# Layer 0's experts with down products five steps behind the up products

## The reference

```python
router_probs = softmax(flat @ router_w + router_b)          # 8 experts
topk_probs, topk_idx = top_k(router_probs, 2)
weights = zeros_like(router_probs).at[rows, topk_idx].add(topk_probs)
shared_out = gelu(flat @ sw1 + sb1) @ sw2 + sb2              # hidden width 256
h1 = gelu(einsum('td,edh->teh', flat, rw1) + rb1)            # all 8 experts
expert_out = einsum('teh,ehd->ted', h1, rw2) + rb2
return shared_out + einsum('ted,te->td', expert_out, weights)
```

## Time and profile before

| | |
|---|---|
| median of 3 runs | 460.7 us |
| profiled execution | 462.43 us, span 460.6 us |
| busy in the span | PE 411.1 (89%), DVE 359.3 (78%), ACT 334.5 (73%), POOL 253.1 (55%) |
| layer 0's experts | 65.8 to about 201 us: tiles of 31.0, 35.4, 35.9 and 32.9 us |
| PE idle in that stage, by its waits | 12 waits for hidl or hidh, 9.8 us together |
| granted TensorE clock over the span | 0.974 |

### The profile page before, as it was taken

The page is one execution under the profiler, slowest core; times in us unless marked ns, Lnnn a source line. Parts: engine busy times, 40 slices in busy tenths (PEclk is TensorE's granted clock), DMA queues, the critical chain, the costliest instruction groups (busy, mean ns, idle before and its releaser), DMA issues.

```text
span 460.6 us, 7995 instructions
## 1 busy us (share of the span) xinstructions
PE 411.1 (89%) x2340; PEld 276.2 (60%) x2340; DVE 359.3 (78%) x891; ACT 334.5 (73%) x898; POOL 253.1 (55%) x276
## 2 busy tenths in 40 slices
PE   8989778899799899889788888979999999999995
PEld 6667566586577667554333333434467787887883
DVE  4768795767898969867988898889966798778763
ACT  4276558798687686677999989999974575675552
POOL 3302238696876677750253446354538875666663
PEclk9899999899999999995999899989999999999999
DMA  6721021131133545561325545421316343432640
GB/s 183 220 74 43 0 76 64 46 95 46 48 113 93 128 122 164 114 109 46 103 47 87 123 116 85 98 74 23 104 27 170 118 138 101 130 114 99 194 123 23
DMA packets 45675, 44.70 MB, mean 97 GB/s; under 512 B 5556, under 2 KB 33788, under 8 KB 45632
## 3 DMA queue, kind: packets, MB, share of 16 engines
q1 hardware_dynamic: 45632, 44.19, 36.1%
HBM read 37.73 MB, written 6.44 MB: 96 GB/s over the span
## 4 chain that ended last, share of the span: by engine, by line
PE 30%; DVE 14%; ACT 7%; DMA 7%; SPq 3%; issue 3%; POOL 1%; POOLq 0%; DVEq 0%; ACTq 0%
PE P L1255 7%; PE P L1257 7%; PE P L1256 7%; DVE nm L911 6%; ACT EX L1192 5%; SPq L342 3%; DMA G<-gate_rows 3%; DMA attention_rows<-O 2%; PE P L1277 2%; PE P L1541 2%; PE P L1529 1%; DMA kv_parts<-kvs 1%; DVE O L926 1%; PE P L1396 1%; DVE kvs L700 1%
## 5 line engine op out<-in xcount | busy, mean ns | idle before, releaser
L470 POOL TENSOR_TENSOR hidl<-tmp,hidh 128x512 fp32r<-128x512 f32 x116 | 149.2, 1294 | 71.8 <-ACT hidh L1144 66.1
L1192 ACT ACTIVATE EX<-P,nm 128x256 f32<-128x256 f32 x256 | 117.2, 509 | 9.0 <-DVE nm L911 8.8
L1144 ACT ACTIVATE hidh<-tmp 128x512 fp32r<-128x512 f32 x116 | 73.1, 630 | 53.4 <-DVE tmp L987 27.9
L911 DVE TENSOR_REDUCE nm<-P 128x4 f32<-128x1024 f32 x64 | 77.9, 1219 | 15.2 <-PE P L1529 14.7
L1255 PE MATMUL P<-XH,WH 128*128 128x512 f32 x176 | 75.8, 431 | 1.3 <-DVE tmp L987 0.9
L1257 PE MATMUL P<-XL,WH 128*128 128x512 f32 x176 | 69.6, 395 | 0.0
L1256 PE MATMUL P<-XH,WL 128*128 128x512 f32 x176 | 69.5, 395 | 0.0
L514 POOL TENSOR_TENSOR qs<-qT,rz 128x128 f32<-128x128 f32 x64 | 25.3, 416 | 73.5 <-DVE rz L919 73.5
L874 DVE TENSOR_TENSOR tmp<-P,G 128x512 f32<-128x512 f32 x64 | 43.4, 686 | 25.9 <-ACT P L1165 15.2
L1192 ACT ACTIVATION_READ_ACCUMULATOR EX<-P,nm 128x1 f32 x256 | 62.2, 243 | 0.0
L1255 PE MATMUL P<-hidh,WH 128*128 128x512 f32 x124 | 50.7, 409 | 11.4 <-POOL hidl L470 9.7
(11 more groups left out here) (140 smaller groups left out, 698.9 us busy)
## 6 DMA issues: line engine op xcount, KB each, us to landing
G<-gate_rows SPq DMA_DIRECT2D x56, 256.0 KB, 3.4
kv_parts<-kvs SPq DMA_DIRECT2D x16, 256.0 KB, 2.9
VS<-kv_parts SPq DMA_DIRECT2D x48, 64.0 KB
KS<-kv_parts SPq DMA_DIRECT2D x48, 64.0 KB
G<-gate_rows SPq DMA_DIRECT2D x8, 224.0 KB, 3.1
G<-gate_rows SPq DMA_DIRECT2D x8, 192.0 KB, 3.2
G<-gate_rows SPq DMA_DIRECT2D x8, 160.0 KB, 2.9
X<-in_x SPq DMA_DIRECT2D x4, 256.0 KB, 3.0
```

Source lines behind the costliest of these rows:

```text
L470: nc.gpsimd.tensor_tensor(hidl[:, u % 3, :], source, hidh[:, u % 3, :].bitcast(fp32), ALU.subtract).then_inc(s["low_ready"], 1)
L911: v.tensor_reduce(nm1[:, g % 4, 2 * h:2 * h + 2, :], P[:, bank:bank + 2, :].rearrange("p j (h s) -> p (j h) s", h=2), AX.X, ALU.max, negat ...
L1144: sc.activation(hidh[:, u % 3, :], source, ACT.Copy).then_inc(s["high_ready"], 1)
L1192: last = sc.activation(ex1(g, j)[:, h * S:(h + 1) * S], P[:, bank_s1(g, j), h * S:(h + 1) * S], ACT.Exp, bias=nm1[:, g % 4, j, h:h + 1], a ...
```

## The change

Five things are changed together.

- Down products of layer 0 stand five steps behind the up products (`LAG0 = 5`); layer 1 keeps 4.
- `hidh` and `hidl` get four blocks in place of three, in both layers; their waits become u-4.
- To make room in SBUF, two small tiles (`gr`, `grt`) move into `WT`, and DVE waits once for the clearing of `WT`.
- Side jobs that hang on the last down product of a tile, or on the shared bank, go one step later: `gate_experts` 3 to 4, `router_logits` 4 to 5, `tokens_back` and `add_experts` 5 to 6.
- In tiles 2 and 3, `project_kv` goes from i=3 to i=1, and DVE's kv jobs from i = 0, 4, 6 to i = 0, 2, 3.

```diff
+LAG0 = 5
-        hidh = sb("hidh", [128, 3, PT], fp32r)
-        hidl = sb("hidl", [128, 3, PT], fp32r)
+        hidh = sb("hidh", [128, 4, PT], fp32r)
+        hidl = sb("hidl", [128, 4, PT], fp32r)
...
+        gr = WT[0:B, 0, 0:2 * D]; grt = WT[0:B, 1, 0:2 * D]
...
             def low_part(u, source):
                 pool.wait_ge(s["high_ready"], u + 1)
-                if u >= 3:
-                    pool.wait_ge(s["down_done"], u - 2)
+                if u >= 4:
+                    pool.wait_ge(s["down_done"], u - 3)
...
             def gate_rows():
                 dve.wait_ge(s["gate_ps"], 1)
+                dve.wait_ge(s["wt_clear"], 1)
...
                 if p + 1 < NP:
-                    if i == 4:
+                    if i == 5:
                         router_logits(0, p + 1)
...
-                    if i == 3:
+                    if i == 4:
                         gate_experts(0, p - 1)
-                    if i == 5:
+                    if i == 6:
                         add_experts(0, p - 1)
...
-                if p >= 2 and i in (0, 4, 6):
-                    kv(TPP * (p - 2) + (1, 2, 3)[i // 3])
+                if p >= 2 and i in (0, 2, 3):
+                    kv(TPP * (p - 2) + (1, 2, 3)[i // 2 + i % 2])
...
             def high_part(u, source):
-                if u >= 3:
-                    act.wait_ge(s["down_done"], u - 2)
+                if u >= 4:
+                    act.wait_ge(s["down_done"], u - 3)
...
-                if u >= LAG:
-                    down0(u - LAG)
+                if u >= LAG0:
+                    down0(u - LAG0)
...
-                    if i == 5:
+                    if i == 6:
                         tokens_back(0, p - 1)
...
-                if p >= 2 and i == 3:
+                if p >= 2 and i == 1:
                     project_kv(2 * p - 3)
...
             scores(0, 0)
-            down0(NP * STEPS0 - 4)
+            for u in range(NP * STEPS0 - 5, NP * STEPS0 - 3):
+                down0(u)
             scores(0, 1)
```

More of the change, by code:

```diff
@@ L133, in two_block_adaln @@
         rn = sb("rn", [128, NT])
-        nm0 = sb("nm0", [128, NT]); warm = sb("warm", [128, 1]); gr = sb("gr", [B, 2 * D]); grt = sb("grt", [B, 2 * D]); Z0 = sb("Z0", [128, NT])
+        nm0 = sb("nm0", [128, NT]); warm = sb("warm", [128, 1]); Z0 = sb("Z0", [128, NT])
         nz = sb("nz", [128, NT])
@@ L467, in low_part @@
                 pool.wait_ge(s["high_ready"], u + 1)
-                if u >= 3:
-                    pool.wait_ge(s["down_done"], u - 2)
-                nc.gpsimd.tensor_tensor(hidl[:, u % 3, :], source, hidh[:, u % 3, :].bitcast(fp32), ALU.subtract
+                if u >= 4:
+                    pool.wait_ge(s["down_done"], u - 3)
+                nc.gpsimd.tensor_tensor(hidl[:, u % 4, :], source, hidh[:, u % 4, :].bitcast(fp32), ALU.subtract
                                         ).then_inc(s["low_ready"], 1)
@@ L1140, in high_part @@
             def high_part(u, source):
-                if u >= 3:
-                    act.wait_ge(s["down_done"], u - 2)
-                sc.activation(hidh[:, u % 3, :], source, ACT.Copy).then_inc(s["high_ready"], 1)
+                if u >= 4:
+                    act.wait_ge(s["down_done"], u - 3)
+                sc.activation(hidh[:, u % 4, :], source, ACT.Copy).then_inc(s["high_ready"], 1)
             act.wait_ge(s["ld_b"], 16 * N_LD["ld_b"])
@@ L1482, in down0 @@
                 pe.wait_ge(s["low_ready"], u + 1)
-                last = split_mm(bank_y0[p], (STEPS0 + block0(i)) * D, D, hidh[:, u % 3, :], hidl[:, u % 3, :],
+                last = split_mm(bank_y0[p], (STEPS0 + block0(i)) * D, D, hidh[:, u % 4, :], hidl[:, u % 4, :],
                                 i == 0, i == STEPS0 - 1)
@@ L1608, in down1 @@
                 pe.wait_ge(s["low_ready"], u + 1)
-                last = split_mm(bank_y1[p], 2 * FP + i * D, D, hidh[:, u % 3, :], hidl[:, u % 3, :],
+                last = split_mm(bank_y1[p], 2 * FP + i * D, D, hidh[:, u % 4, :], hidl[:, u % 4, :],
                                 i == 0, i == C1 - 1)
```

## The result

Four executions of the changed kernel gave 466.03, 469.37, 471.3 and 472.33 us, median 470.3; four of the kernel before, on the same chip, 458.28 to 461.1, median 460.5. The ratio is 1.022, with a 95% interval of 1.016 to 1.028: slower by 9.8 us. Forecast were +3.4 us, 464 us, with a range up to 468.5. A second set gave the changed kernel 465.2 us (10 executions, 461.79 to 470.36) against 460.0 (25): ratio 1.011, interval 1.0058 to 1.0163, +5.2 us. So the sign is sure and the size differs from set to set. Ratios are meant without executions that are more than 1.5% above the fastest of their kernel; where counting all of them changes a reading, the text gives both. The profiled execution of the first set took 466.03 us (forecast for it: 465.8), but that is partly chance: the stage began 2.0 us earlier than before, and was 6.3 us longer.

The account below looks back on a forecast made before the run. The stage was taken as bound by several engines in turn (PE, DVE, ACT). Tiles 0 to 3 gave -1.2 - 0.2 + 4.0 + 0.8 = +3.4 us, so 464 us by the median, range 457.8 to 468.5.

Parts of the forecast that it names:

- what the lag gives: Tiles 0 and 1: PE's waits for `hidl` shrink with lag 5, tile 0 by -1.2 us, tile 1 by -0.2.
- the 0.70 I had set as a limit for one: Each PE wait for a low part can shrink by at most 0.70 us, one more up product ahead of it.
- the latency from `kvs` to `tmp`(2): Tiles 2 and 3: `tmp`(2) comes 2.7 us after `kvs` releases `project_kv` at i=1, in tile 2 at 141.8 instead of 139.1.
- the clock lost behind the two at i=1 is hidden in the next wait: Tiles 2 and 3: lower clock after the waits at `project_kv` costs nothing; only that behind `tokens_back` counts.
- half clock: Rival, chance 0.13: PE at half clock behind the two `tokens_back` waits, 1.8 us each, 467.5 us.
- the two kv jobs ahead of the logits: Tile 2, DVE: two kv jobs (4.5 us) make `tmp`(2) to logits 9.4 us, gelu(7) +4.5, the tile +4.0.
- The PE wait in `tokens_back`: PE waits 2 to 4 us there, for `ld` in tile 2 and yT in tile 3.
- tile 3's relief: Tile 3: i=7 starts +4.4 us, three `hidl` waits save 2.5, the G wait of 3.59 is absorbed; +0.8 in all.
- The held G load: End of tile 3: SP's G load starts at about 191.8 again; DVE's 3.59 us wait for it goes into PE's delay.
- The rival that the jobs run unobstructed: Rival, chance 0.17: kv jobs meet no POOL low part, take 1.2 us each; sum +0.5, 461.2 us, no change.
- The rival "the lag pays": Rival, chance 0.25: new PE waits fall into time it waited later anyway, only relief is left; -3.3, 457.4 us.

Follow-up runs that it names:

- k1: The changed kernel with its kv jobs back at their old places (`project_kv` at i=3, DVE's at i = 0, 4, 6); 457.28 us in twelve executions, ratio 0.9958.
- p1: The changed kernel with only DVE's kv jobs back at i = 0, 4, 6, `project_kv` left at i=1; 465.8 us, ratio 1.0119.
- f1: The changed kernel with filler matmuls, results unread, ahead of `project_kv` at i=1 and ahead of `tokens_back`; 462.8 us, ratio 1.0051.
- the fair pair of profiles: One profile of the kernel before and one of the unedited changed kernel, second set; tiles 0 to 3 sum to 135.3 and 138.5 us.

## Why the prediction was off

**Right: what the lag gives.** The waits for `hidl` were to shrink and PE to stand at W. Tile 0 got 2.0 us shorter (forecast -1.2, bounds -3 to 0): 1.0 of it stays where the lower clock falls into the tile, as it did before (30.0 in k1, p1 and f1); the other 1.0 comes only where it does not. Its wait shrank by 1.3 us, more than the 0.70 I had set as a limit for one; why is not shown, but PE had stood 2.1 us at route instead, where before it stood 1.85 at the down product behind. Tile 1 got 0.6 longer (forecast -0.2, bounds -1.5 to +2), with the lower clock in it in both profiles; where it is absent, tile 1 with lag 5 is 35.1 (once 35.9), so -0.3 to +0.5. Together the two are -1.4, as forecast, but the clock has a hand in both, and that the sum fits is in part luck.

**Right: the latency from `kvs` to `tmp`(2).** Forecast was 2.7 us from release to `tmp`; at whole clock it is 2.67 in tiles 2 and 3 alike. In tile 2 PE's wait came out at 2.77 instead of 3.9, since the kv jobs ahead of it ended 5.8 us into the tile and not 6.9; in tile 3 it is the 2.40 of the forecast. p1 shows that PE's job at i=1 is the costly half of the move: 5.2 us in tiles 2 and 3 together, against k1.

**The first step that failed: "the clock lost behind the two at i=1 is hidden in the next wait".** I gave half clock a chance of 0.13, as a rival on top, and priced it only behind `tokens_back`. It was a term of the sum. The pair of profiles of one kernel shows its size: half clock behind `kvs` in tile 2 costs 1.46 us in full (37.58 to 39.04), because `tmp`(2) waits for just these matmuls, and DVE has nothing else; behind yT in tile 3 it costs 1.6 (i=7 to i=17 in 18.74 us against 17.11). The stretch in tile 1 was not hidden either: both profiles of the changed kernel have it, and the tile is 36.1 us with it and 35.1 (once 35.9) without. With the two of tiles 2 and 3, the second profile's +3.3 comes to +6.4; the first profile shows +6.3. That its three sister executions took 469 to 472 us at clocks down to 0.956 agrees with more of it, but they were not traced, so the remainder of the 9.8 us is not laid to any place.

**The second: the two kv jobs ahead of the logits.** From `tmp`(2) to the end of the logits I had 9.4 us, 4.5 of them two kv jobs, and put gelu(7) 4.5 later by it. It took 7.5: the jobs took 1.9 and 1.4 us, not 2.25 each (in tile 3 3.0 and 2.3). And even these did not lengthen tile 2: p1, which has both behind yT and one of them behind the logits, has nearly the same length (37.8 against 37.6), since DVE then idles where they would be. The exp did start with the end of the logits, but also with the end of ACT's high part; in p1, where the logits end 0.09 us ahead of it, it comes right behind the high part, and no sooner after `kvs` (10.6 us against 10.2). So what holds tile 2 back is PE's wait at i=1; the jobs' time, on which I had put most of it, is not seen in its length. Tile 2 at whole clock was +1.7 and not +4.0. The PE wait in `tokens_back` is 0.90, not 2 to 4.

**The third: tile 3's relief.** I had its up product i=7 at +4.4 (measured +5.0), and then took 2.5 us off for three `hidl` waits. At whole clock only 1.3 came (18.40 to 17.11), with `project_q` waiting 1.1 us for XT where it had not waited. The held G load was still late as well: its issue is at 193.89 and not 191.8, since the kv loads ahead of it begin at 189.72, 2.5 us later than the earlier trace rows has them; in the second profile DVE waits 2.18 us for it at `tmp`(16). But `tmp`(17), with which the tile ends, waited for ACT's gelu after that (0.53 us), so the load is not what came last. Together tile 3 is +2.9 at whole clock in place of +0.8. In tiles 2 and 3 the errors in size nearly cancel (+4.6 against +4.8), which is why the sum of +3.4 fits the second profile's +3.3; it should not be read as five good terms.

**The kv jobs beside POOL.** The rival that the jobs run unobstructed was half true in tile 2. DVE and POOL, changed kernel, first profile:

```profile
132.83 1.30 POOL L472 TENSOR_TENSOR hidl<-wmod,hidh 128x512 fp32r<-128x512 f32 x1
133.50 0.78 DVE L702 CAST kvs<-kvf 128x256 fp32r<-128x256 f32 x1
...
171.87 1.26 POOL L472 TENSOR_TENSOR hidl<-wmod,hidh 128x512 fp32r<-128x512 f32 x1
171.95 1.46 DVE L703 TENSOR_TENSOR kvs<-kvf,kvs 128x256 fp32r<-128x256 f32 x1
```

Beside the low part of 171.87 the subtraction takes 1.46 us, about as long as that; the one at 134.31 begins when POOL's instruction has ended and takes 0.43, while the cast ahead of it, which had begun beside it, takes 0.78. That agrees with the rule of the Trainium skill, GPSIMD Engine Reference, section Specifications, that the SBUF interface is shared with VectorE, with contention for instructions with two SBUF inputs. The cast has one SBUF input, so for it the rule would need a 2-port mode, which no run here shows. But it did not give "no change": the 2.7 us from `kvs` to `tmp`(2) is a latency and has nothing to do with the price of a job.

**The rival "the lag pays" was half right.** Without the kv part, lag and rings together pay, by 1.9 us (k1: 457.3 against 459.2), not the 3.3 I had allowed; as much waiting as went came back under other names. The fourth block alone gave 0.9965 against k1's 0.9958, so how much of it is the lag's is open. I had let this rival fail on the jobs; it fails on PE's wait.

**What stays open.** Why the same waits at the same places leave the clock whole in one execution and halved in the next; how much the DVE half of the kv part costs by itself over many executions (p1's ratio and the changed kernel's are equal within their intervals, at equal clock p1 is 1.3 to 2.4 us lower, and the tiles of one profile each say 0.8); where the 4.5 to 6 us at equal clock lie, of which the fair pair of profiles shows 3.3 in the stage; and why the stage starts at 63.8 us in one profile of the changed kernel and at 65.7 in the other (in k1 at 67.2 and 65.3).

## What to carry to other kernels

A wait put into the queue of an engine that the stage hangs on costs its own length: here 2.9 us for 2.4 us more of waiting and 5.2 for 4.6. One place further back it was cheaper only because PE reached it later. Jobs moved on an engine that has gaps (DVE in tile 2) may cost nothing, so ask of each engine whether it would stand idle there anyway. A deeper lag needs its ring blocks (lag 5 with three cost 30 us), moves waits to the next dependence rather than removing them, and is judged by the tile's length, not by the wait that vanished. Idle PE time on the path carries a second price, the lower clock behind it, that may or may not come in a given execution: put it into the sum with a range, and compare tiles at like clocks and at like places, not at like times of two profiles.

## What the hardware showed unexpectedly

- One program, one place, waits equal to 0.01 us: granted clock 0.57 in a 4 us window of one profile and 1.00 in the other (134 to 138 us, which holds the end of a wait of 2.8 us for `kvs` in both). The four matmuls behind that wait took 2.08 us in the one and 1.13 in the other.
- More matmuls in the same 142 us (593 records, against 558 in k1) did not lengthen the stage: fillers in waits cost nothing that the tiles show, and the clock stayed at 1.00.
- A stretch at the lower clock lengthened tile 0 by 1.0 us, tile 2 by 1.5 and tile 3 by 1.6 between profiles with the same jobs in the tile.
- Executions of the same program spread by 3% (458.66 to 472.27 in p1), and in the kernel before the spread goes with the mean granted clock, which no edit of the program set (correlation -0.78).
- The same DVE subtraction with both inputs in SBUF took 0.42 or 1.46 us, and a cast 0.29 or 0.78; the long ones had a POOL low part under way beside them.
